# Layer 1's experts on tiles of 128 routed rows instead of on all tokens

## What is computed

```python
probs = softmax(flat @ gate_W)
topk_w, topk_idx = top_k(probs, 2)
topk_w = topk_w / topk_w.sum(axis=-1, keepdims=True)
combine = (one_hot(topk_idx, 8) * topk_w[..., None]).sum(axis=1)
out = 0.5 * gelu(flat @ shared_W + shared_b)
for e in range(8):
    h = gelu(flat @ W1[e] + b1[e])                        # 128 -> 512
    out = out + combine[:, e:e+1] * (h @ W2[e] + b2[e])   # 512 -> 128
out = layernorm(out) * gamma + beta
```

## Time and profile before

| | us |
|---|---|
| median of three runs | 1377.84 |
| lowest and highest | 1374.54, 1380.12 |
| the profiled execution | 1381.02 |
| its span, first to last instruction | 1378.9 |
| TensorE busy (8072 products) | 1260.3 |
| DVE busy | 806.1 |
| ACT busy | 684.0 |
| POOL busy | 321.4 |
| mean granted TensorE clock, of full speed | 0.948 |

### The profile page before, as it was taken

The page is one execution under the profiler, slowest core; times in us unless marked ns, Lnnn a source line. Parts: engine busy times, 40 slices in busy tenths (PEclk is TensorE's granted clock), DMA queues, the critical chain, the costliest instruction groups (busy, mean ns, idle before and its releaser), DMA issues.

```text
span 1378.9 us, 24109 instructions
## 1 busy us (share of the span) xinstructions
PE 1260.3 (91%) x8072; PEld 870.1 (63%) x8072; DVE 806.1 (58%) x2043; ACT 684.0 (50%) x1163; POOL 321.4 (23%) x505
## 2 busy tenths in 40 slices
PE   4999999999999995559799999999999999999996
PEld 2223333323333332558689899899898898998885
DVE  3777878867788858687733633645436336333322
ACT  1266767656676773214343545345534434455532
POOL 3113141313213121331400500503304105003110
PEclk8599999979999997789899999999999999999998
DMA  5231230303122100800000000000000000000000
GB/s 164 66 101 38 65 93 11 101 3 100 28 74 73 31 3 4 242 25 5 3 9 1 7 12 1 7 12 4 17 1 5 15 1 7 12 2 12 1 12 8
DMA packets 35500, 47.50 MB, mean 34 GB/s; under 512 B 5743, under 2 KB 25392, under 8 KB 35256
## 3 DMA queue, kind: packets, MB, share of 16 engines
q1 hardware_dynamic: 35384, 46.03, 12.0%
HBM read 34.88 MB, written 10.65 MB: 33 GB/s over the span
## 4 chain that ended last, share of the span: by engine, by line
PE 53%; DVE 3%; issue 1%; ACT 1%; POOL 0%; DMA 0%; POOLq 0%; ACTq 0%; DVEq 0%
PE ps_o L1634 16%; PE ps_z L1620 5%; PE a L1700 4%; PE ps_z L1622 4%; PE ps_z L1621 4%; PE a L1710 4%; PE a L1686 4%; PE b_ L1646 3%; PE a L1663 3%; PE a L1641 2%; DVE gsel L1433 1%; PE b_ L1641 1%; PE b_ L1757 1%; DVE sel L1406 1%; PE b_ L1731 1%
## 5 line engine op out<-in xcount | busy, mean ns | idle before, releaser
L594 DVE TENSOR_REDUCE nmax<-ps_s 128x1 f32<-128x512 f32 x512 | 324.5, 682 | 83.0 <-PE ps_s L761 81.9
L488 ACT ACTIVATE p_ring<-ps_t 128x512 f32<-128x512 f32 x512 | 287.1, 597 | 146.4 <-PE ps_t L772 140.5
L1242 ACT ACTIVATE hid<-ps_z,b 128x512 f32<-128x512 f32 x256 | 176.0, 688 | 303.4 <-PE ps_z L1622 302.9
L1634 PEld LDWEIGHTS ps_o<-w,hid 128*128 128x128 f32 x2048 | 257.5, 192 | 23.1 <-issue 8.0
L1634 PE MATMUL ps_o<-w,hid 128*128 128x128 f32 x2048 | 260.8, 276 | 2.5 <-ACT hid L1242 0.8
L761 PE MATMUL ps_s<-k_stack,q_stack 72*128 72x512 bf16 x512 | 207.2, 407 | 12.7 <-DMA q_stack<-q_parts_dram 8.1
L772 PE MATMUL ps_t<-q_stack,k_stack 75*128 75x512 bf16 x512 | 199.5, 392 | 6.9 <-ACT p_ring L488 3.9
L761 PEld LDWEIGHTS ps_s<-k_stack,q_stack 72*128 72x128 bf16 x512 | 51.2, 100 | 161.3 <-DVE nmax L594 104.9
L783 PE MATMUL ps_av<-p_ring,v_ext 128*32 128x512 f32 x1024 | 139.1, 616 | 0.0
L1620 PE MATMUL ps_z<-hTf_high,w_high 128*128 128x512 f32 x256 | 122.2, 477 | 3.3 <-issue 2.5
L1441 DVE COPY y<-a 128x128 f32<-128x128 f32 x64 | 18.4, 288 | 179.3 <-PE a L1700 179.3
(11 more groups left out here) (239 smaller groups left out, 1630.4 us busy)
## 6 DMA issues: line engine op xcount, KB each, us to landing
k_stack<-k_parts_dram SPq DMA_DIRECT2D x32, 288.0 KB
q_stack<-q_parts_dram SPq DMA_DIRECT2D x32, 288.0 KB
q_parts_dram<-q_parts SPq DMA_DIRECT2D x40, 128.0 KB, 2.3
k_parts_dram<-k_parts SPq DMA_DIRECT2D x24, 128.0 KB, 2.3
w<-in_w SPq DMA_DIRECT2D x1, 2048.0 KB, 9.3
hid<-in_w SPq DMA_DIRECT2D x2, 1024.0 KB
out_x<-x_done SPq DMA_DIRECT2D x8, 256.0 KB, 2.4
gates<-gates_dram SPq DMA_DIRECT2D x1, 1024.0 KB, 4.3
```

Of the source, the lines that this page charges most:

```text
L488: nc.scalar.activation(probs[:, u % RING, :], ps_t[u % TBANKS][:], ACT.Exp, scale=HD ** -0.5).then_inc(exp_done, 1)
L594: nc.vector.tensor_reduce(nmax[:, js, n:n + 1], ps_s[u % SBANKS][:], AX.X, ALU.max, negate=True).then_inc(max_done, 1)
L1242: nc.scalar.activation(hid1[e % 2][:, n, :], ps_z[q % 2][:], ACT.Gelu, bias=b1[:, e, n:n + 1]).then_inc(hid1_ready, 1)
L1634: last = nc.tensor.matmul(ps_o[:, quarter(t)], hid1[e % 2][:, f, quarter(t)], w2_1[:, e, f, :], start=(f == 0), stop=(f == NF - 1))
```

## The change

Layer 1's experts leave the stages. The new kernel runs them after all stages, on 72 tiles of 128 rows, each row being one (token, choice) pair routed to one expert: 8192 pairs fill 64 tiles, and eight more cover the partly filled ones.

- **Lists.** A DRAM tensor `rows` has a region of 4096 rows for each expert (33792 rows of 130 numbers: 128 normed features, the row's target in `back`, its weight). During the attention program POOL fills it with empty rows, three of 24 parts in each of eight batches, 17.6 MB in all.
- **Router.** A stage's own batch is now routed one stage later than its attention. DVE marks first and second choice, TensorE counts ranks with small bf16 products (`ranks`), DVE makes slots (`find_slots`) and rows (`fill_rows`), and POOL sends 128 rows at a time with eight indirect transfers per batch. The modulation of the normed rows moves from ACT to two POOL operations.
- **Tiles.** A table on DVE gives each tile its expert and first row. For each tile SP loads a register and the 128 rows (66 KB), TensorE transposes them, makes the hidden product in plain f32 (4 products of 128 columns), ACT applies gelu, TensorE makes the output (4 products), DVE multiplies it with the row's weight, and POOL writes it to `back` with an indirect transfer. DVE also loads a register with the expert's number and copies that expert's weights (128 x 1028 numbers) from one resident tensor to one of three buffers.
- **End.** For each batch the two results of every token are loaded, added to the part that all tokens share (`base`), normed, gated and stored.
- Each stage now works on attention of batch b + 1, the router of batch b and layer 0's experts of batch b + 2; the split of the weights is gone; there are ten stages instead of eleven, of which seven have both layer 0's experts and layer 1's attention.

```diff
+TILES = 2 * NBLOCK + E
+XT, WT = 4, 3
@@ POOL, attention program
+                    nc.gpsimd.dma_start(
+                        scratch["rows"].ap().rearrange("(p a n) c -> p a (n c)", p=P, a=FILLS)[:, bass.ds(n * b, n), :],
+                        empty.unsqueeze(1).to_broadcast([P, n, FILL_ROWS * ROW])
+                    ).then_inc(emptied, 16)
@@ POOL, stages
-            def split_w1():
...
+                if it.route:
+                    pool.wait_ge(slot_ready, b + 1)
+                    pool.wait_ge(row_ready, b + 1)
+                    settle(pool)
+                    for k in range(2):
+                        for t in range(NT):
+                            nc.gpsimd.indirect_dma_start(
+                                out=scratch["rows"].ap(),
+                                out_offset=bass.IndirectOffsetOnAxis(ap=slot[:, k, t:t + 1], axis=0),
+                                in_=hrow[:, k, t, :], in_offset=None).then_inc(sent, 16)
...
+                    nc.gpsimd.tensor_tensor(xh_f[:], xh_f[:], over_tokens(mod_f[:, 0, :]), ALU.mult).then_inc(hf_step, 1)
+                    pool.wait_ge(hf_step, nxt + 1)
+                    nc.gpsimd.tensor_tensor(hrow[:, 0, :, 0:D], xh_f[:], over_tokens(mod_f[:, 1, :]), ALU.add
+                                            ).then_inc(hf_ready, 1)
@@ SP, tiles
+            for j in range(TILES):
+                if j >= XT:
+                    sp.wait_ge(tt_filled, j - XT + 1)
+                    sp.wait_ge(yt_ready, j - XT + 1)
+                    sp.wait_ge(target_ready, j - XT + 1)
+                start = sp.value_load(start_of[j:j + 1, 0:1], min_val=0, max_val=HROWS - P)
+                sp.dma_start(xt[j % XT][:], scratch["rows"].ap()[bass.ds(start, P), :]).then_inc(xt_in[j % XT], 16)
@@ POOL, tiles
+            for j in range(TILES):
+                pool.wait_ge(yt_ready, j + 1)
+                pool.wait_ge(target_ready, j + 1)
+                nc.gpsimd.indirect_dma_start(
+                    out=scratch["back"].ap(),
+                    out_offset=bass.IndirectOffsetOnAxis(ap=target[j % XT][:, 0:1], axis=0),
+                    in_=yt[j % XT], in_offset=None, bounds_check=2 * B * T - 1, oob_is_err=False
+                ).then_inc(y_sent[j % XT], 16)
@@ DVE, order in the stages
                 if it.ffn:
+                    if it.attn:
+                        work[0] += [lambda: select(nn, 0), lambda: split_a(nn)]
...
+                    for q, f in ((9, shift_logits), (11, shared), (13, best_two), (13, combine), (15, fill_rows),
+                                 (18, find_slots), (20, start_base)):
@@ DVE, tiles
+            def copy_weights(j):
+                if j >= WT:
+                    dve.wait_ge(yt_filled, j - WT + 1)
+                e = dve.value_load(expert_of[j:j + 1, 0:1], min_val=0, max_val=E - 1)
+                nc.vector.tensor_copy(wtile[j % WT][:], wall[:, bass.ds(e, 1), :].rearrange("p e n -> p (e n)")
+                                      ).then_inc(wt_ready, 1)
+            copy_weights(0)
+            copy_weights(1)
+            for j in range(TILES):
+                dve.wait_ge(xt_in[j % XT], 16 * (j // XT + 1))
+                if j >= XT:
+                    dve.wait_ge(y_sent[j % XT], 16 * (j // XT))
+                nc.vector.tensor_scalar(target[j % XT][:], xt[j % XT][:, D:D + 1], 2e6, None, ALU.min
+                                        ).then_inc(target_ready, 1)
+                dve.wait_ge(yt_filled, j + 1)
+                nc.vector.tensor_scalar(yt[j % XT], ps_y[j % 2][:, 0:D], xt[j % XT][:, D + 1:D + 2], None, ALU.mult
+                                        ).then_inc(yt_ready, 1)
+                if j + 2 < TILES:
+                    copy_weights(j + 2)
@@ TensorE, tiles: tile_hidden and tile_output are four products of 128 columns each
+            tile_T(0)
+            tile_T(1)
+            tile_hidden(0)
+            for j in range(TILES):
+                if j + 2 < TILES:
+                    tile_T(j + 2)
+                if j + 1 < TILES:
+                    tile_hidden(j + 1)
+                tile_output(j)
```

More of the change, by code:

```diff
@@ L17 @@
 F32R = mybir.dt.float32r
+I32 = mybir.dt.int32
 ALU = mybir.AluOpType
@@ L920, in _, with __init__ @@
             pipeline(pe, iteration)
[L923 to L928, removed]
+class Stage:
+    def __init__(self, own, ffn=True, ffn_next=True, attn=True, attn_next=True, route=True):
+        self.own, self.ffn, self.ffn_next = own, ffn, ffn_next
+        self.attn, self.attn_next, self.route = attn, attn_next, route
 def program_experts(nc, io, keep, scratch, held):
@@ L969, in program_experts @@
         half = sb("half_b", [P, NT])
[L971 to L978, removed]
+        earlier = sb("earlier", [P, P])
+        earlier_b = sb("earlier_b", [P, P], BF16)
+        ones_b = sb("ones_b", [P, P], BF16)
+        region = sb("region", [P, E])
+        block_rows = sb("block_rows", [P, NBLOCK])
+        tile_no = sb("tile_no", [P, 2])
+        ids = sb("ids", [P, B, 2, NT])
         st_a = sb("st_a", [P, NT, 6])
@@ L1153, in iteration @@
                     gate_rows(gate0[:], 2, 1, nn, gate0_in)
-                if it.after and it.later:
+                if it.attn_next and it.attn:
                     sp.wait_ge(xb1_ready, nxt + 1)
@@ new lines, in last_add @@
+            def last_add(m):
+                pool.wait_ge(outg_ready, m + 1)
+                if m >= 2:
+                    pool.wait_ge(stored[m % 2], 16 * (m // 2))
+                if m == 0:
+                    pool.wait_ge(xb2_ready, B)
+                nc.gpsimd.tensor_tensor(x_done[m % 2], xh_o[m % 2], x_all[:, m], ALU.add).then_inc(out_ready, 1)
+            both(0)
+            for m in range(B):
+                spread(m)
+                if m + 1 < B:
+                    both(m + 1)
+                last_add(m)
@@ L1583, in iteration @@
+                if it.ffn and not it.route:
                     for n in range(ROUNDS // 2):
                         work[6 + 3 * n].append(lambda n=n: take_last(ROUNDS // 2 * (b + 2) + n))
-                    if it.after:
+                    if it.attn:
+                        work[29].append(save_earlier)
                         work[28].append(lambda: rank_taken(nc, rows, is_taken, rank, best_taken, rank_step, rank_ready))
                         work[31].append(place_last)
-                if it.later:
+                if it.ffn:
@@ new lines, in sums, with normalised @@
+            def sums(m):
+                dve.wait_ge(both_ready, m + 1)
+                nc.vector.tensor_tensor(base[:, m], base[:, m], back[m % 2][:, :, 0, :], ALU.add).then_inc(sum_ready, 1)
+                dve.wait_ge(sum_ready, m + 1)
+                statistics(base[:, m], st_o, mv_o, sto_done, mvo_done, m, xho_ready)
+            def normalised(m):
+                dve.wait_ge(rso_ready, m + 1)
+                if m >= 2:
+                    dve.wait_ge(out_ready, m - 1)
+                for t in range(NT):
+                    last = nc.vector.tensor_scalar(xh_o[m % 2][:, t, :], base[:, m, t, :], mv_o[:, t, 0:1],
+                                                   rs_o[m % 2][:, 1, t:t + 1], ALU.subtract, ALU.mult)
+                last.then_inc(xho_ready, 1)
+                dve.wait_ge(xho_ready, m + 1)
+                nc.vector.tensor_tensor(xh_o[m % 2], xh_o[m % 2], over_tokens(gate_end[:, 0, m, :]), ALU.mult
+                                        ).then_inc(outg_ready, 1)
@@ L1802, in iteration @@
+                if it.attn and not it.route:
                     work[30].append(place_last)
-                if it.later:
+                if it.ffn:
                     work[3].append(lambda: gather(0))
```

692 lines of the change are left out of this document (413 added, 279 removed).

## The result

| | us |
|---|---|
| before, median of four executions (1374.54 to 1380.12) | 1377.72 |
| changed, median of four (1472.46 to 1477.72) | 1476.13 |
| ratio, 95% interval | 1.0712 (1.0682 to 1.0742) |
| profiled execution of the changed kernel | 1472.46, span 1470.8 |
| forecast | 1535 (1410 to 1650) |

The direction and the range held, and the size was 60 us too high: 157 us were forecast to be lost, 98 were.

What follows compares the result with a forecast made beforehand. TensorE, busy 91% of the span, was taken as the bound. Span 599.7 + 2 + 413 + 72 (two last stages) + 7 (loop entry) + 378 + 64 = 1536 us, adjusted to 1535; range 1410 to 1650.

Steps and rivals of the forecast that it cites:

- Attention program and fill, +2 us: Attention program: POOL's zero fills mostly fit its idle time and add 2 us; bounds 0 and 8 x 4 us.
- First stage: Up to the first gating: POOL's split gone, -10.7 us; selection and split moved behind the gating, -3.5; closes at 599.7.
- S = 59 us: Length of each of seven stages with layer 0's experts in the new order, 413 us in all; bounds 52 and 67.
- The price of a send, 1.2 us: POOL's eight indirect writes per stage: 1.2 us each, 10 us per stage; bounds 0.46 and 3 us each.
- Which fits behind the router: In each stage, POOL's 10 us of sends fit beside some 18 operations of about 1 us in 59 us.
- The tile loop's chain, 3.2 + V: One tile turn: hidden 0.89, output 1.06, y_j 0.29, register load V, weight copy 0.69, signals about 0.2 us.
- the copies run ahead: Rival in the tile loop: copies not held behind y_j, 2.3 us a tile, 1323 us total; faster cases 0.08.
- V = 1.1 us: Tile loop: wait before the weight copy, the later of DVE's register load and POOL's indirect write, taken as 1.1 us.
- The clock, T = 5.25 instead of 4.3: Tile loop: middle of 4.3 us a turn at full clock and 6.2 at 1.2 GHz; 72 tiles take 378 us.
- 1467 us with V = 1.1, 1402 with V near nothing: Rival: full clock holds in the tile loop, turns of 4.3 us, or 3.4 with V near nothing; chance 0.25.
- End, 64 us: After the tile loop: write and load back 8 us, eight batches of 6.4, addition and store 5; bounds 50 and 80.
- Break-even: Tile loop turn at which the kernel equals the one before: 3.07 us per tile, with 1157 us outside the loop.

Runs made afterwards that it cites:

- experiment 6: Changed kernel with the load of ids issued ahead of layer 0's two weight loads on SP's queue: 1455.7 us, ratio 1.058.
- experiment 4: Changed kernel without the eight indirect sends per stage, each tile's y stored by a plain transfer: 1419.0 us (one execution).
- experiment 5: Changed kernel with only the first choice's four sends per stage, y stored by a plain transfer: 1430.1 us (one execution).
- experiment 9: experiment 2, experiment 6 and experiment 7 combined, plus POOL waiting for four sends to land before issuing the other four: 1318.0 us, ratio 0.958.
- Experiments 1: Changed kernel with VectorE copying tile j+2's weights before it waits for tile j's output: 1406.9 us, ratio 1.023.
- experiment 3: Changed kernel with each weight row copied twice in the tile loop, lengthening the pause in a turn: 1614.7 us (one execution).
- experiment 7: Changed kernel with SP issuing the end's load of batch m+1 before waiting to store batch m-1: 1466.6 us, ratio 1.068.
- experiment 2: Changed kernel with weights copied before the output wait and eight buffers instead of four for rows and results: 1359.1 us, ratio 0.990.
- experiment 11: experiment 9 plus the next batch's first selection and split made late in the stage before: 1291.5 us, ratio 0.938.

## Why the prediction was right and wrong, step by step

- *Attention program and fill, +2 us*: right. The second program starts 1.8 us later.
- *First stage*: the 11.8 us beside POOL's split went as said. The step that failed is one that the sum does not contain: ids was added to the semaphore on which VectorE waits, at the tail of SP's queue. 19 us; experiment 6 gives it back (18.4 us of the stage, 20 of the median).
- *S = 59 us*: 63.2 on average, 64.5 with a router. The first expert product came 15.2 to 17.5 us after the gating, 16 were forecast. The price of a send, 1.2 us, is right too (0.96 and 0.30 between two). "Which fits behind the router" is the step that failed: not through POOL's time, but because TensorE's signals came late while more than four sends were out (7.3 us a stage by experiment 4, of which 6.8 by experiment 5 go with the second four; experiment 9 gives back 3.8). Without them a stage takes 57.2, and S = 59 stands near it.
- *The tile loop's chain, 3.2 + V*: right in its links, and close in their prices. The links as listed add up to 3.13, which the prediction wrote as 3.2; measured they are 3.20 (hidden 0.96 instead of 0.89, y_j 0.35 instead of 0.29), and with the 0.40 of the register load 3.60. Experiments 1 and 2 show it, and so does the rival "the copies run ahead": once they do, a tile takes 2.02 us and the kernel is faster than before.
- *V = 1.1 us*: the mis-sized term. Two reasons were given for it, and neither holds: the register load leaves a gap of 0.40 us, and POOL's write does not shut out the copy. The Trainium skill, "DMA: Bandwidth & Descriptors", section "Latency and other measured facts", gives about 0.6 us for such a load; here it is less.
- *The clock, T = 5.25 instead of 4.3*: experiment 3 bears out the step (5.55 on average), but not its input. One of its three rows was misread: between 36 and 40 TensorE is busy for all of the 4.00 us, so that stretch shows the lower clock and no pauses. The middle was a choice between two levels for which the prediction had no reason, so that it came near 5.55 is luck. An error of 0.7 us in V made 1.65 us of T, 119 us in all, because the second step doubled the first: at 3.60 us the granted clock stays at 0.99. The forecast named this case as a rival (1467 us with V = 1.1, 1402 with V near nothing), and gave it 0.25. The part to which it gave most (1480 to 1580, 0.37) was missed by 4 us, and that 1476 lies well inside the wider range is owed to the parts that were too low, which made up for half of the loop.
- *End, 64 us*: 74.6. The 6.4 us a batch counted DVE's and POOL's operations and not the load that waits for the store of the batch before (7.7 in most batches; experiment 7, 6.34).
- *Break-even*: with the other parts as measured (1470.8 - 259 = 1211.8) the loop must stay under (1378.9 - 1211.8) / 72 = 2.3 us a tile. The experiments lie on both sides of it as they should: 2.64 is slower, 2.02 faster.

## What to carry to other kernels

Write down the closed chain of a loop before its busy times: here a copy for tile j+2 stood behind the result of tile j on an engine that takes its instructions in order, and three weight buffers were worth nothing until the two changed places. Then ask what is late next (the row load was), and give every ring the depth of the faster turn. When a load is added to a semaphore that somebody already waits for, its place in the queue becomes theirs. And where one uncertain term decides the clock, work out the sum at both ends of the term: at 0.40 us for V the loop was 259 us, and the middle of the two levels described no loop with that V.

## What the runs showed of the hardware

- Signals of TensorE were held back for 3.6 to 6.5 us in the full stages of the changed kernel, while eight indirect writes of 128 rows were issued 1.26 us apart; with four in a stage they were not (experiment 5), and with a wait for the first four to land mostly not (one wait of ScalarE of 2.4 us in experiment 9, four of 2.3 in experiment 11). Why is open: the runs show when it happens and not where the signals stay. A signal the other way came in time in the same stretch: ScalarE's gelu ended at 918.10 and TensorE's output product began at 918.20.
- A POOL write of indices and a VectorE copy. The Trainium skill, "SBUF — State Buffer", section "Who interferes with whom", has both take one port pair, exclusively. On the timeline of the kernel of experiment 2, one copy begins within POOL's f32 addition (1150.75) and the next within a write (1152.64):

```profile
1150.41 1.30 POOL L1367 TENSOR_TENSOR x<-x,w 128x512 f32<-128x512 f32 x1
1150.75 1.52 DVE L1806 COPY wtile<-wall 128x1028 f32 x1 [0.33 <-issue]
...
1151.88 1.59 POOL L1360 DMA_INDIRECT back_dram<-w,target  x1 [0.16 <-issue]
...
1152.64 0.70 DVE L1806 COPY wtile<-wall 128x1028 f32 x1
```

  The addition makes the copy 1.52 us long instead of 0.70, as the rule says. The write does not: the copy takes its 0.70 us, and the write grows from 0.96 to 1.59. Of 14 copies of this kernel that began within a write, 13 took 0.69 to 0.71 us (one 0.87). The write took 1.52 to 1.61 us in the eight cases in which the copy began 0.70 to 0.79 us into it, and 0.97 to 0.98 in the six in which it began earlier. So of the two it was mostly the write that grew, and only where the copy came late in it.
- With a pause of 2.1 us in every turn the granted clock went back and forth between its two levels, 0.59 to 0.84 in stretches of 20 us (experiment 3); with a pause of 1.48 us it stayed at 0.99 (the changed kernel).
